# A decoder layer with an eight-expert FFN on one core: rows sorted by pair of experts, finished tile by tile

## What is computed

```python
logits = einsum('btd,ed->bte', x, Wr);  probs = softmax(logits)
topk_vals, topk_idx = top_k(probs, 2)
gate = topk_vals / topk_vals.sum(-1), at the two chosen of E = 8 experts
h = silu(einsum('btd,efd->btef', x, W1))          # DFF = 512
y = einsum('btef,edf->bted', h, W2)
x = layernorm(x + einsum('bte,bted->btd', gate, y))
```

## Time and profile before

| | |
|---|---|
| median of three runs | 1378.03 us |
| the profiled execution | 1379.32 us |
| its span, first to last instruction | 1377.4 us |
| mean granted clock of TensorE in it | 0.858 |
| PE / weight loads busy | 962.4 / 815.0 us |
| VectorE / ACT / POOL busy | 857.2 / 729.5 / 445.7 us |
| bytes moved | 73.7 MB, mean 54 GB/s |

### The profile page before, as it was taken

The page is one execution under the profiler, slowest core; times in us unless marked ns, Lnnn a source line. Parts: engine busy times, 40 slices in busy tenths (PEclk is TensorE's granted clock), DMA queues, the critical chain, the costliest instruction groups (busy, mean ns, idle before and its releaser), DMA issues.

```text
span 1377.4 us, 30644 instructions
## 1 busy us (share of the span) xinstructions
PE 962.4 (70%) x10082; PEld 815.0 (59%) x10083; DVE 857.2 (62%) x2598; ACT 729.5 (53%) x1364; POOL 445.7 (32%) x535
## 2 busy tenths in 40 slices
PE   4888888884999999999997402111698977676740
PEld 2777777773888888888886301000587866555530
DVE  3688888885788888888885730000454666566552
ACT  3666766653776767767763300000575765555531
POOL 3123333332010010010102357777002055654555
PEclk8989998887999999999997555555799999899985
DMA  6930000000001000000000002111233334443431
GB/s 193 290 87 15 15 15 15 15 9 18 13 11 21 10 11 17 10 19 10 0 1 1 1 38 71 51 59 52 55 93 86 92 95 106 99 107 99 101 87 53
DMA packets 157233, 73.72 MB, mean 54 GB/s; under 512 B 76034, under 2 KB 151042, under 8 KB 157188
## 3 DMA queue, kind: packets, MB, share of 16 engines
q1 hardware_dynamic: 148996, 56.34, 15.6%
q0 software_dynamic: 8192, 16.79, 4.2%
HBM read 22.76 MB, written 37.75 MB: 44 GB/s over the span
## 4 chain that ended last, share of the span: by engine, by line
PE 38%; DVE 22%; issue 21%; ACT 13%; another core or an unknown queue 2%; POOL 2%; DMA 1%; DVEq 1%; ACTq 0%; SPq 0%; POOLq 0%
PE bank L449 9%; PE bank L451 8%; PE bank L450 8%; PE bank L551 4%; DVE at L925 4%; DVE X L1002 3%; ACT XTa L746 3%; DVE mx L909 3%; ACT qzh L746 3%; PE bank L537 3%; PE bank L528 2%; DVE st L992 2%; ACT vz_self L755 1%; DVE z L937 1%
## 5 line engine op out<-in xcount | busy, mean ns | idle before, releaser
L424 POOL DMA_INDIRECT wst<-yd,pos x128 | 129.9, 1015 | 222.2 <-DVE z L1117 105.6
L449 PE MATMUL bank<-XTa,qzh 128*128 128x128 f16 x768 | 146.0, 226 | 37.7 <-ACT XTa L746 37.7
L925 DVE TENSOR_TENSOR at<-bank,rc 64x32 f32<-64x32 f32 (+1 forms) x768 | 153.5, 200 | 14.4
L831 ACT ACTIVATE pr<-bank 128x512 f32<-128x512 f32 x96 | 57.3, 597 | 192.4 <-remote 106.5
L760 ACT ACTIVATE pr<-bank 128x512 f32<-128x512 f32 x192 | 114.1, 594 | 79.5 <-PE bank L528 78.3
L909 DVE TENSOR_REDUCE mx<-bank 128x8 bf16<-128x512 f32 x192 | 132.9, 692 | 28.7 <-PE bank L451 23.1
L451 PE MATMUL bank<-XTa,qzl 128*128 128x128 f16 x768 | 146.5, 226 | 0.0
L450 PE MATMUL bank<-XTa,qzh 128*128 128x128 f16 x768 | 146.3, 226 | 0.0
L764 ACT ACTIVATE pt<-bank 128x512 f32<-128x512 f32 x192 | 113.3, 590 | 60.5 <-PE bank L537 60.1
L411 POOL DMA_INDIRECT xd<-XTa,pos x128 | 123.8, 968 | 65.3 <-issue 65.3
L1098 DVE TENSOR_TENSOR xtl<-xs,xth 128x512 f16<-128x512 f32 x96 | 66.4, 695 | 120.4 <-ACT xth L832 71.5
(11 more groups left out here) (202 smaller groups left out, 3084.5 us busy)
## 6 DMA issues: line engine op xcount, KB each, us to landing
yd<-at SPq DMA_DIRECT2D x96, 128.0 KB
xd<-blank SPq DMA_DIRECT2D x2, 3072.0 KB, 20.7
X<-x_dram SPq DMA_DIRECT2D x16, 256.0 KB, 2.8
wst<-w_dram SPq DMA_DIRECT2D x16, 256.0 KB, 2.7
xd<-blank SPq DMA_DIRECT2D x1, 4096.0 KB, 28.3
cin<-ctx_in_dram SPq DMA_DIRECT2D x16, 256.0 KB, 2.8
out_dram<-z SPq DMA_DIRECT2D x16, 256.0 KB
xd<-blank SPq DMA_DIRECT2D x1, 2048.0 KB, 21.5
```

Source lines behind the costliest of these rows:

```text
L424: nc.gpsimd.indirect_dma_start(out=yg[k][:, t, :], out_offset=None, in_=yd[chunk_of(n)], in_offset=bass.IndirectOffsetOnAxis(ap=pos[k][:, ...
L449: nc.tensor.matmul(out_, lh, rh, start=start, stop=False, **kw)
L831: nc.scalar.activation(s32[n % 4][:], bank[n % 4][:], ACT.Silu, scale=IWS)
L925: m = nc.vector.tensor_tensor(dst, src, r, ALU.mult)
```

## The change

Tokens are sorted by their pair of experts instead of by expert. PAIRS lists the 28 pairs (a, b) with a < b; a token goes into one list, so its row is sent once: 64 indirect DMAs. The row grows to 528 bytes (ROW = 264 f16), with its two gates and its token number behind the 256 halves; a filler row has the number TOK. There is one memory xd, no chunks: SP waits for all 64 scatters before it fetches a tile.

There are NTILE = 92 tiles of 128 rows, four to a turn (NJ = 23), each with two expert numbers in the word. PE does both experts for each, up into the four H banks (two banks a tile: 512 columns for each expert), down into 256 columns of one of four Y banks. ACT and VectorE work on the two banks of a tile at once, 1024 columns. Beside the transposed tiles SP loads the same rows untransposed (`load_rows`), of which POOL's `take` makes the residual by adding the halves, and keeps the token numbers. VectorE adds gate times product for both experts onto it (`mix`) and takes the statistics (`spread`, `moments`); POOL's `give` makes the inverse deviation, scales four tiles and scatters each by token numbers straight to the output, filler rows falling outside the bounds. yd, the gathers, the evictions, the stores and ACT's scaling are gone. Several buffers are laid together or over others' memory.

```diff
-RT = 256
-CHUNKS = ((0, 16), (16, 40), (40, 56), (56, 64))
...
+PAIRS = [(a, b) for a in range(E) for b in range(a + 1, E)]
+NP = len(PAIRS)
+NTILE = 4 * ((TOK // P + NP - 1 + 3) // 4)
 NJ = NTILE // 4
...
+PB = NP // 4 * NT
+ROW = 2 * D + 8
...
+            def turn(j, i):
+                for m in range(2):
+                    wait_apart(sp, f_h, 4 * j + 2 * m + 2, ld_w, 96)
+                    load(2 * j + m + 4, 2 * i + m)
+                wait_apart(sp, f_z, 4 * j + 4, ld_w, 96)
+                wait_apart(sp, f_id, j + 1, ld_w, 96)
+                load_rows(j + 2, i)
...
+            for t in range(NT):
+                if t % SEG == 0 and t >= 2 * SEG:
+                    pool.wait_ge(sent[t // SEG - 2], 16 * SEG)
+                nc.gpsimd.indirect_dma_start(out=xd, out_offset=bass.IndirectOffsetOnAxis(ap=pos[:, t:t + 1], axis=0),
+                                             in_=rows_out[:, t, :], in_offset=None).then_inc(sent[t // SEG], 16)
...
+                for k in range(4):
+                    if not first_group(j):
+                        wait_apart(pool, put[k], 16 * j, pool_ready, POOL_READY)
+                    nc.gpsimd.tensor_scalar(zo[k], zr[i][:, k, :], mv[:, k, 0:1], rstd[:, k:k + 1], ALU.subtract, ALU.mult).then_inc(f_fin, 1)
...
+                for k in range(4):
+                    nc.gpsimd.indirect_dma_start(out=out_rows, out_offset=bass.IndirectOffsetOnAxis(ap=dest[:, k:k + 1], axis=0), in_=zo[k],
+                                                 in_offset=None, bounds_check=TOK - 1, oob_is_err=False).then_inc(put[k], 16)
+                if more:
+                    take(j + 2, i)
...
-            nc.tensor.matmul(bank[3][:], tri[:], M16[:], start=True, stop=True)
-            nc.tensor.matmul(bank[4][:], ones2[:, 0:P], M16[:], start=True, stop=True).then_inc(r_rank, 1)
+            for n in range(4):
+                nc.tensor.matmul(bank[n][:, 0:PB], tri[:], M16[:, n * PB:(n + 1) * PB], start=True, stop=True)
+                nc.tensor.matmul(bank[4 + n][:, 0:PB], ones2[:, 0:P], M16[:, n * PB:(n + 1) * PB], start=True, stop=True).then_inc(r_rank, 1)
...
+            def up(q, e, base):
+                r = slice(q % 2 * P, q % 2 * P + P)
+                for f in range(FC):
+                    w = base[e] + f * 2 * P
+                    m = three(H[(2 * q + e) % 4][:, f * P:(f + 1) * P], (W1[:, bass.ds(w, P)], W1[:, bass.ds(w + P, P)]),
+                              (xt[q // 2][:, 0, r], xt[q // 2][:, 1, r]), start=f == 0, skip_group_check=True)
...
+            def down(i, q, base):
...
+                for e in range(2):
+                    for f in range(FC):
+                        c, w = slice((FC * e + f) * P, (FC * e + f + 1) * P), base[e] + f * 2 * P
+                        for l in range(2):
+                            nc.tensor.matmul(y[:, e * P:(e + 1) * P], sh[q % 2][:, c], W2[:, bass.ds(w + l * P, P)],
+                                             start=e == 0 and f == 0 and l == 0, stop=False, skip_group_check=True)
+                pe.wait_ge(f_sl, i + 1)
...
+                    act.wait_ge(f_h, 4 * j + k + 1)
+                    nc.scalar.activation(sh[n][:], h, ACT.Silu, scale=IWS).then_inc(f_si, 1)
+                    nc.scalar.activation(s32[n], h, ACT.Silu, scale=IWS).then_inc(f_s, 1)
...
+            nc.vector.tensor_tensor(M16.rearrange("p (c t) -> p c t", t=NT), rt[:, 0].unsqueeze(1).to_broadcast([P, NP, NT]),
+                                    code.unsqueeze(2).to_broadcast([P, NP, NT]), ALU.is_equal).then_inc(r_m, 1)
...
+                link(nc.vector.tensor_tensor_scan(runs[:, b], wipe[:, b], bank[4 + n][:, 0:PB], 0.0, ALU.mult, ALU.add))
...
+                link(nc.vector.tensor_tensor(runs[:, b], runs[:, b], bank[n][:, 0:PB], ALU.add))
...
+            link(nc.vector.scalar_tensor_tensor(out=runs_c, in0=start.unsqueeze(2).to_broadcast([P, NP, NT]), scalar=float(P), in1=runs_c,
+                                                op0=ALU.mult, op1=ALU.add))
+            link(nc.vector.tensor_tensor(runs, runs, M16, ALU.mult))
+            link(nc.vector.tensor_reduce(rt[:, 0], runs.rearrange("p (c t) -> p t c", t=NT), AX.X, ALU.add))
...
+                nc.vector.scalar_tensor_tensor(out=z4, in0=bank[4 + q % 4][:, e * P:(e + 1) * P], scalar=row_gate[q // 4][:, q % 4, e:e + 1],
+                                               in1=z4, op0=ALU.mult, op1=ALU.add).then_inc(f_z if e else f_a, 1)
```

More of the change, by code:

```diff
@@ L316, in _ @@
+            for n in range(NT // SEG):
+                sp.wait_ge(sent[n], 16 * SEG)
+            for k in range(2):
+                load(k, k)
+            load_rows(0, 0)
+            for k in range(2, 4):
+                load(k, k)
+            load_rows(1, 1)
+            turn(0, 0)
+            with sp.Fori(0, (NJ - 3) // 2) as j:
+                turn(2 * j + 1, 1)
+                turn(2 * j + 2, 0)
         @block.gpsimd
@@ L686, in four, with turn @@
+            def turn(j, half, word, last):
+                base = offsets(word, 0)
                 for k in range(4):
-                    i, follow = 4 * j + k, not (last and k == 3)
+                    i, q, follow = 4 * j + k, 4 * half + k, not (last and k == 3)
+                    if k == 3 and follow:
+                        word = carried()
                     if follow:
-                        ahead = offset(word, k + 1)
-                        pe.wait_ge(ld_t[(k + 1) % 4], 16 * (j + 1 + (k + 1) // 4))
@@ L691, in four @@
-                    for c in range(2):
-                        if follow:
-                            up((k + 1) % 4, c, ahead)
-                        if k == 2 and c == 0 and not last:
-                            pe.reg_mov(experts, load_word(j + 1))
-                        down(i, k, c, base)
+                        ahead = offsets(word, (k + 1) % 4)
+                        if k % 2 == 1:
+                            pe.wait_ge(ld_t[(q + 1) // 2 % 4], 8 * (j - half) + 16 * ((q + 1) // 8) + 16)
@@ L697, in four @@
+                        for e in range(2):
+                            up((q + 1) % 8, e, ahead)
+                    if k == 1 and not last:
+                        pe.reg_mov(pairs, load_word(j + 1))
+                    down(i, q, base)
                     base = ahead
-            def carried():
-                return pe.snap(experts, min_val=0, max_val=E ** 5 - 1)
             pe.wait_ge(r_tab, 1)
@@ L705, in _ @@
             pe.wait_ge(ld_t[0], 16)
[L706 to L712 removed]
+            first = offsets(word, 0)
+            for e in range(2):
+                up(0, e, first)
+            turn(0, 0, word, False)
+            with pe.Fori(0, (NJ - 3) // 2) as j:
+                turn(2 * j + 1, 1, carried(), False)
+                turn(2 * j + 2, 0, carried(), False)
+            turn(NJ - 2, 1, carried(), False)
+            turn(NJ - 1, 0, carried(), True)
         @block.scalar
```

510 lines of the change are left out of this document (211 added, 299 removed).

## The result

| | before | after |
|---|---|---|
| median of 20 runs each | 1383.3 us | 1374.6 us |
| lowest to highest | 1376.46 to 1390.51 | 1369.24 to 1379.8 |
| profiled execution / its span | 1379.32 / 1377.4 us | 1375.59 / 1373.6 us |
| mean granted clock of TensorE | 0.858 | 0.876 |

The ratio is 0.994, interval 0.9923 to 0.9958: 0.6% faster. I had forecast 1384 and called slower the likeliest, at 0.50. The time lies within the wide range of 1343 to 1415, but it moved the other way. (The kernel before had 1378.03 as the median of three; over twenty runs it is 1383.3.)

A forecast was written before the change was run, and what follows sets the result against it. PE's sequencer, not the array, was taken to bound the undisturbed tiles. Span 894.7 + 3 + 434.7 + 2 + 35 + 13.2 = 1382.6 us, with 1.9 outside it 1384.5, forecast as 1384; range 1343 to 1415.

The forecast's parts named there:

- Routing, sending, PE's start: Before the tiles: first scatter starts at about 809.1 us, last at 889.2, PE starts at 894.7, or 897.7 with 3 added.
- the 3 us for a rest of the crawl: At PE's start: 3 us allowed for slow matmul issue left over after the last scatter.
- Rival E: At PE's start: its first 13 us go at 2.8 us a matmul, giving 1393 us; chance 0.05.
- 23 turns of 18.9 us: Expert tiles, four a turn: 16.0 us of weight addresses plus 2.9 us remainder, 434.7 us in all.
- "Bursts" at 1.6 us each: Output scatters beside PE's tiles: each of 22 bursts of four POOL DMAs stops PE for 1.6 us, 35 us together.
- Rival C: Output scatters: bursts cost PE nothing, so 35 us fall away, 1349 us; chance 0.17.
- Rival D: Output scatters: bursts cost double, up to 3.2 us each, 1404 to 1419 us; chance 0.18.
- The tail: From PE's last matmul to the last scatter's landing: 13.2 us, for 47 before.
- Covers: Within a turn: ACT, VectorE and POOL work hides under 18.9 us, POOL taking 10.3, its loop with VectorE 13.
- My own case: Whole kernel: the forecast's own account with the sequencer as bound, 1374 to 1395 us; chance 0.55.
- The crawl of 120 us: Kernel before, about 852 to 976 us: PE's instruction supply is slow while POOL issues scatters, costing some 120 us.
- Rival B: Expert tiles: weight addresses hide, a tile takes 2.64 us plus loads, POOL's loop bounds at 13.1 a turn, 1214; chance 0.05.

## Why the prediction was wrong, step by step

- **Routing, sending, PE's start.** Right within 2 us: 811.2 for 809.1, 890.9 for 889.2, 896.5 for 897.7. The last agrees better than its parts: sending ended 1.7 us late, and the 3 us for a rest of the crawl were not there. Rival E fell.
- **23 turns of 18.9 us.** Right in kind, 0.4 us short: 19.33 in the mean of two steady turns without scatters. Address records come at 0.124 us, 32 a tile; I had cut the remainder of the turn from 3.4 to 2.9, and it stayed at 3.3. With the first and last turn the tiles came out 7.5 us longer.
- **"Bursts" at 1.6 us each.** The step that failed, with its row. The earlier trace rows show PE's gap and a burst of gathers, and I took one for the other's effect. It was VectorE's own queue. Measured 0.45 us a burst, 9.8 us for my 35: 25 us too much, which turned the sign. Rival C is the nearer one (it decides below 1.1 us), but its zero and its 1349 missed too, and its reason, reading against writing, was wrong; I gave it 0.17. Rival D, twice the price, fell.
- **The tail.** 13.8 for 13.2. But I ended the sum at the last landing; the 9.3 us of the drain behind it, which lay under other work in the kernel before, I had put at nothing without asking.
- **Covers.** ACT and VectorE lie hidden, shown by the run of 512 columns. POOL's turn was 13.4 us and not 10.3 (four scalings 4.1 to 4.2 instead of the 2.2 that I had derived from the 512-wide one of the earlier trace rows; even with VectorE idle four take 3.1), hidden here, and the bound as soon as the sequencer was relieved.
- **Why the total is near even so.** By luck. With the bursts at their size the sum would have been 1359, faster by over 1%; the turns (7.5 us) and the drain (9.3 us) that I had too short brought it back to 1376. My own case reached down to 1374, but for other reasons.
- **The crawl of 120 us.** There in the trace before the change and in every later one that sends rows beside PE's tiles, except the one at 1228 us. The same scatters run beside PE there without a crawl, so "while POOL issues scatters, PE's own instruction supply is slow" is not the whole cause: something outside the program must come in, and which is open. (The 14 of 110 us that I quoted for the crawl belong to 790 to 900, half of which lies before PE's start.)
- Rival B fell by the two runs with fewer addresses. The Trainium skill, "Advanced Engine Details and Errata", section "Sequencer Loop", says that other engine instructions can be read and queued while a control instruction executes in microcode. Here 32 addresses less took 4.1 to 4.2 us off a turn with the same columns, so in this loop they do not hide.

## What to carry to other kernels

When an engine's gap is labelled "issue" and keeps step with another engine's burst, look first whether its next instruction waits on a third engine, and list what stands ahead of the awaited work in that engine's queue. Where weights are addressed by a register, count addresses as well as columns: twice the width at the same address was worth 61 us here. And repeat the kernel before: a time that depends on something outside the program can be larger than the change.

## What the runs showed of the hardware

- A weight address in PE's sequencer costs 0.124 us where they follow each other: 32 fewer took a turn from 19.38 to 15.15 us (later, in the versions without steps of 0.7 us, from 19.15 and 19.50 to 15.04 and 15.43).
- With POOL's indirect DMAs running, PE's instructions may come 0.7 us or a multiple of it apart, for 120 us (kernel before) or once or twice in a turn (changed kernel), and in other executions of the kernel before not at all (1228 us). With 1.4 us or more between pairs of DMAs no step was seen in two traces, one of them from the comparison in which the kernel before took 1228 us.
- POOL's closing drain took 1.63 to 1.64 us in the kernel before and its variants, 5.30 us in the run without scatters and 8.892 us in all others, and 12 us of other work before it changed nothing.
- POOL's scaling of 128 columns took 0.78 us at the end, with VectorE idle, and 1.03 in the mean of all; in the run with four additions a tile 1.12 in the mean and 1.24 in the turns at 1024 and 1041 us.
